# A two-layer graph attention kernel: four of twelve heads turned by TensorE instead of DMA, in a new order of steps

## The reference

```
layer 0: q,k,v = x@Wq+bq, x@Wk+bk, x@Wv+bv          (6 heads of 64)
         p = softmax(q@k.T/sqrt(64) + mask);  y = (p@v)@Wf + bf
         x1 = layernorm(x + y)
layer 1: h = x1@W (12 heads of 32);  th = tanh(h)
         z[i,j] = leaky(th@w_src[i] + th@w_dst[j]);  masked -> -999
         f = elu(softmax(z)@h + b);  g = sigmoid(x1@Hw.T + Hb)
         out = layernorm(x1 + g*f + (1-g)*x1)
```

## Time and profile before

| | |
|---|---|
| three runs | 1217.51, 1220.42, 1220.64 us; median 1220.42 |
| profiled execution | 1217.34 us, span 1215.6 us, mean granted clock 0.974 |
| busy shares of the span | PE 90%, PEld 80%, POOL 82%, ACT 80%, DVE 79% |
| chain that ended last | PE 56%, POOL 15%, issue 14%, DVE 11%, ACT 2%, DMA 1% |
| DMA engines' busy share | 31% |

### The profile page before, as it was taken

One profiled execution on the slowest core, in us unless ns is written; L12 is line 12 of the kernel. 1 busy time (PEld: TensorE's weight loads), 2 busy tenths in 40 slices (PEclk: granted clock), 3 DMA queues, 4 the chain that ended last, 5 costly groups with the idle time before them and its releaser, 6 DMA issues.

```text
span 1215.6 us, 35318 instructions
## 1 busy us (share of the span) xinstructions
PE 1091.1 (90%) x12234; PEld 975.3 (80%) x12297; DVE 962.6 (79%) x1948; ACT 968.6 (80%) x1868; POOL 1000.1 (82%) x813
## 2 busy tenths in 40 slices
PE   4689999999999999999999999999999999999851
PEld 4578888888888888888888888888888888888741
DVE  5567888888888888888888888888888888888843
ACT  5258888888888888888888888888888888888854
POOL 1138898888989888889988888988888898988876
PEclk9799999999999999999999999999999999999975
DMA  4103332223333222333322233332223333223233
GB/s 144 43 17 83 81 90 65 73 68 93 87 86 92 66 68 67 93 87 87 93 66 66 68 93 89 85 93 66 66 74 87 93 87 86 73 67 75 68 66 79
DMA packets 244762, 95.18 MB, mean 78 GB/s; under 512 B 223349, under 2 KB 239738, under 8 KB 244730
## 3 DMA queue, kind: packets, MB, share of 16 engines
q1 hardware_dynamic: 244730, 94.76, 31.2%
HBM read 31.22 MB, written 12.58 MB: 36 GB/s over the span
## 4 chain that ended last, share of the span: by engine, by line
PE 56%; POOL 15%; issue 14%; DVE 11%; ACT 2%; DMA 1%; DVEq 1%; SPq 0%; POOLq 0%; ACTq 0%
PE lin L448 33%; PE zp L545 6%; POOL z L1295 5%; POOL prod L1254 5%; PE fp L570 3%; PE zp L603 3%; PE zp L607 3%; DVE sd L978 2%; PE fp L620 2%; PE fp L573 2%; PE tp L487 2%; DVE y L1073 1%; DVE f L1117 1%; DVE z L1098 1%; ACT th L721 1%
## 5 line engine op out<-in xcount | busy, mean ns | idle before, releaser
L1302 POOL TENSOR_TENSOR p_lo<-z,p_hi 128x1536 f16<-128x1536 f32 x64 | 200.9, 3139 | 0.0
L1295 POOL TENSOR_TENSOR z<-z,z_max 128x1536 f32<-128x1536 f32 x64 | 176.5, 2758 | 9.1 <-DVE z_max L1105 6.1
L784 ACT ACTIVATE z<-zp 128x1536 f32<-128x1536 f32 x64 | 93.1, 1455 | 85.9 <-PE zp L607 85.9
L1254 POOL TENSOR_TENSOR prod<-th,w_sd_rows 128x768 f32<-128x768 f32 x64 | 120.5, 1883 | 14.0 <-ACT th L721 14.0
L620 PE MATMUL fp<-h_part,p1t_hi 128*128 128x33 bf16 x2304 | 110.6, 178 | 19.2 <-DMA p1t_lo<-p_lo 14.8
L620 PEld LDWEIGHTS fp<-h_part,p1t_hi 128*128 128x128 f16 x2304 | 104.4, 96 | 27.2 <-issue 24.1
L1307 POOL TENSOR_TENSOR f<-f,x_kept 128x384 f32<-128x384 f32 x64 | 64.7, 1011 | 73.6 <-DVE f L1124 69.4
L1098 DVE SCALAR_TENSOR_TENSOR z<-zp,z 128x1536 f32<-128x1536 f32 x64 | 112.2, 1753 | 11.0 <-ACT z L784 8.3
L776 ACT ACTIVATE p<-p,p_min 128x128 f32<-128x128 f32 x384 | 118.9, 396 | 0.0
L1105 DVE TENSOR_REDUCE z_max<-z 128x12 f32<-128x1536 f32 x64 | 111.6, 1744 | 0.0
L623 PE MATMUL fp<-h_part,p1t_lo 128*128 128x33 bf16 x1536 | 106.8, 178 | 0.0
(11 more groups left out here) (161 smaller groups left out, 4387.0 us busy)
## 6 DMA issues: line engine op xcount, KB each, us to landing
xt_raw<-x_t SPq DMA_DIRECT2D x32, 384.0 KB, 3.4
x_raw<-x SPq DMA_DIRECT2D x32, 384.0 KB, 3.5
out<-out_tile SPq DMA_DIRECT2D x64, 192.0 KB, 1.9
adj<-adj SPq DMA_DIRECT2D x64, 32.0 KB, 2.8
dst_row<-sd_t SPq DMA_DIRECT2D x64, 9.0 KB
p1t_hi<-p_hi SPq DMA_TRANSPOSE x64, 3.3
p1t_lo<-p_lo SPq DMA_TRANSPOSE x64, 3.3
z<-Wq SPq DMA_DIRECT2D x1, 576.0 KB, 3.5
```

Source lines behind the costliest of these rows:

```text
L784: act.activation(z[:, g, :], zp[:, :, :].rearrange("p b n -> p (b n)"), ACT.Copy)\
L1254: pool.tensor_tensor(prod[:, g, :].rearrange("p (s d) -> p s d", s=2), th[:, g:g + 1, :].to_broadcast([128, 2, D]), rows["w_sd"][:, :].rea ...
L1295: pool.tensor_tensor(zs, zs, z_max[:, g, :].unsqueeze(2).to_broadcast([128, H1, N]), ALU.subtract)\
L1302: pool.tensor_tensor(p1_lo[:, g, :], z[:, g, :], p1_hi[:, g, :], ALU.subtract).then_inc(w1_lo[g].sem, 1)
```

## The change

- Heads 0 to 3 (512 of the 1536 columns) of each graph are transposed by TensorE straight from the float32 weights `z` (`weights1_transposes`, into a `tp` bank), and split on eviction: `turned1_high` on ACT, `turned1_low` on DVE. Heads 4 to 11 go on as before, so `weights1_high`, `weights1_low` and both DMA transposes handle 1024 columns instead of 1536.
- `attend1(g, 0)` waits for `turned1_low`, and `attend1(g, 1)` for the DMAs.
- `z_copy` of the next pair also waits until the transposes have read `z`.
- The step lists of all five engines are in another order, and the banks have other users. On PE `queries_keys(0)` now runs ahead of the late attention steps, `hidden(1)` follows `attend1(0, 2)`, and `gate_rows(0)` is late.

```diff
+PE_HEADS, DMA_HEADS = 4, 8
-LIN_USERS = ("qk0", "pr0", "pr1", "g1", "v0", "qk1", "qk2", "v1", "h0", "h1", "g0")
-TP_USERS = ("pt11", "pt10", "ct0", "ct1", "x1t0", "x1t1", "pt00", "pt01", "sdt")
+LIN_USERS = ("h1", "qk0", "g0", "pr0", "g1", "pr1", "v0", "qk1", "qk2", "v1", "h0")
+TP_USERS = ("pt01", "pt00", "pt11", "sdt", "pt10", "ct0", "ct1", "x1t0", "wt0", "wt1", "x1t1")
-SECOND_BANK = ("pr0", "pr1", "v0", "qk2", "h0", "g0", "pt10", "ct1", "pt00", "pt01")
+SECOND_BANK = ("h1", "g0", "pr0", "g1", "v0", "qk2", "h0", "pt01", "pt11", "ct0", "ct1", "x1t0", "wt1")
...
+                def weights1_transposes(g):
+                    pe.wait_ge(z_exp[g].sem, prev(z_exp[g]))
+                    bank_free(TP_USERS, f"wt{g}")
+                    bank = tp_bank(f"wt{g}")
+                    for i in range(PE_HEADS):
+                        last = pe.transpose(bank[:, N * i:N * (i + 1)], z[:, g, N * i:N * (i + 1)], ident[:, :])
+                    last.then_inc(wt_mm[g].sem, 1)
...
                     if k == 0:
...
+                        pe.wait_ge(wt_lo[g].sem, now(wt_lo[g]))
+                    if k == 1:
                         pe.wait_ge(wt_turned[g].sem, prev(wt_turned[g]))
...
+                    act.wait_ge(wt_mm[g].sem, now(wt_mm[g]))
                     act.activation(z[:, g, :], zp[:, :, :].rearrange("p b n -> p (b n)"), ACT.Copy)\
...
-                    act.activation(p1_hi[:, g, :], z[:, g, :], ACT.Copy).then_inc(w1_hi[g].sem, 1)
+                    act.activation(p1_hi[:, g, :], z[:, g, PE_HEADS * N:], ACT.Copy).then_inc(w1_hi[g].sem, 1)
+
+                def turned1_high(g):
+                    act.wait_ge(wt_mm[g].sem, now(wt_mm[g]))
+                    act.wait_ge(f_mm[g].sem, prev(f_mm[g]))
+                    act.activation(p1t_hi[:, g, 0:PE_HEADS * N], tp_bank(f"wt{g}")[:, :], ACT.Copy)\
+                        .then_inc(wt_hi[g].sem, 1)
...
+                def turned1_low(g):
+                    dve.wait_ge(wt_hi[g].sem, now(wt_hi[g]))
+                    dve.wait_ge(f_mm[g].sem, prev(f_mm[g]))
+                    dve.tensor_tensor(p1t_lo[:, g, 0:PE_HEADS * N], tp_bank(f"wt{g}")[:, :],
+                                      p1t_hi[:, g, 0:PE_HEADS * N], ALU.subtract).then_inc(wt_lo[g].sem, 1)
```

More of the change, by code:

```diff
@@ L626, in attend1 @@
                         last.then_inc(f_mm[g].sem, 1)
+                turn.late(2, attend1, 0, 2)
+                turn.late(1, hidden, 1)
+                turn.late(0, weights0_transposes, 0, 1)
+                turn.late(0, weights0_transposes, 0, 0)
+                turn.late(2, attend1, 1, 0)
+                turn.late(2, attend1, 1, 1)
                 turn.late(2, attend1, 1, 2)
+                turn.step(0, queries_keys, 0)
                 turn.late(0, weights0_transposes, 1, 1)
+                turn.late(1, gate_rows, 0)
+                turn.late(1, source_target_transposes)
+                turn.late(0, attend0, 0)
                 turn.late(0, weights0_transposes, 1, 0)
-                turn.late(0, attend0, 0)
+                turn.late(0, context_transposes, 0)
                 turn.late(1, attention1, 0)
                 turn.late(0, attend0, 1)
-                turn.late(0, context_transposes, 0)
-                turn.step(0, queries_keys, 0)
+                turn.late(0, project, 0)
                 turn.late(0, context_transposes, 1)
-                turn.late(0, project, 0)
                 turn.late(1, attention1, 1)
+                turn.late(1, gate_rows, 1)
                 turn.late(0, project, 1)
-                turn.late(1, gate_rows, 1)
                 turn.step(0, values, 0)
+                turn.step(1, x1_transposes, 0)
                 turn.step(0, queries_keys, 1)
                 turn.step(0, queries_keys, 2)
-                turn.step(1, x1_transposes, 0)
                 turn.step(0, values, 1)
+                turn.step(2, weights1_transposes, 0)
                 turn.step(0, scores, 0)
+                turn.step(2, weights1_transposes, 1)
                 turn.step(1, hidden, 0)
@@ L843, in next_x_high @@
                                    xt_raw[:, :, :].rearrange("p c n -> p (c n)"), ACT.Copy).then_inc(xt_hi_made.sem, 2)
+                turn.late(1, z_copy, 0)
+                turn.late(1, gate_quarter, 0)
                 turn.step(0, queries_keys, 0)
+                turn.late(0, context_high, 1)
+                turn.late(1, hidden_part1, 1)
+                turn.late(1, hidden_part2, 0)
                 turn.late(1, z_copy, 1)
                 turn.late(1, keep_x1, 0)
-                turn.late(1, hidden_part2, 1)
[L849 to L863, removed]
+                turn.late(1, keep_x1, 1)
+                turn.late(1, gate_tanh, 1)
+                turn.late(0, norm0, 0)
+                turn.step(0, value_part1, 0)
+                turn.step(1, x1_high, 0)
+                turn.late(1, z_exponent, 0)
+                turn.step(0, queries_keys, 1)
+                turn.late(1, weights1_high, 0)
+                turn.step(0, queries_keys, 2)
+                turn.late(1, z_exponent, 1)
+                turn.late(1, weights1_high, 1)
+                turn.step(2, turned1_high, 0)
+                turn.late(0, norm0, 1)
+                turn.step(0, value_part1, 1)
+                turn.step(2, turned1_high, 1)
+                turn.late(1, hidden_part2, 1)
                 turn.step(1, hidden_tanh, 0)
                 turn.step(1, x1_high, 1)
+                turn.step(-1, next_x_high)
                 turn.step(0, scores_exp, 0)
-                turn.step(0, value_part2, 1)
+                turn.step(0, value_part2, 0)
                 turn.step(1, hidden_tanh, 1)
+                turn.step(0, weights0_high, 0, 1)
                 turn.step(0, weights0_high, 0, 0)
@@ L1146, in shift_norm1 @@
                         .then_inc(norm1_shift[g].sem, 1)
+                turn.late(0, weights0_low, 1, 0)
+                turn.late(0, context_low, 0)
+                turn.late(2, elu, 1)
+                turn.late(0, context_inverse, 1)
                 turn.late(0, context_norm, 1)
                 turn.late(1, z_leak, 0)
-                turn.late(0, context_low, 0)
-                turn.late(2, elu, 1)
-                turn.late(1, z_maxima, 0)
+                turn.step(0, queries_keys, 0)
+                turn.late(0, add_residual, 0)
                 turn.late(0, context_low, 1)
-                turn.late(0, add_residual, 0)
-                turn.step(0, queries_keys, 0)
                 turn.late(0, stats0, 0)
@@ L1158, in body @@
                 turn.late(0, variance0, 0)
+                turn.late(1, z_maxima, 0)
+                turn.late(0, shift_norm0, 0)
                 turn.late(1, z_leak, 1)
@@ L1203, in body @@
                 turn.late(2, shift_norm1, 1)
-                turn.step(0, context_inverse, 1)
             turns(dve, passed, body, other_weights)
```

127 lines of the change are left out of this document (59 added, 68 removed).

## The result

The changed kernel takes 1210.01 us (median of 4, 1209.52 to 1211.80) against 1219.49 for the kernel before on the same chip: ratio 0.9927, 95% interval 0.9908 to 0.9945. It is faster by 0.7%. The prediction said 1230 and slower, with 0.67; its own range, 1222 to 1244, lies above the time, and only the wide one, 1200 to 1259, holds it.

What follows compares the result with a forecast made beforehand. PE was taken to set the 35.3 us turn: less 2.1, plus 0.9, 0.86 and 0.8, gives 35.8. Over 30 turns +13.5, less 3 at the end: 1227.8 profiled, about 1230 median; own range 1222 to 1244, wide 1200 to 1259.

Steps and rivals of the forecast that it cites:

- The four old stalls: PE's waits before source_target_transposes, attend0(0), project(0) and values(0), 1.44 us a turn as marked, were all to go.
- together 2.1 us a turn: Worth of PE's four old stalls: 1.44 us marked, plus about 0.16 more for each.
- PE has no idle to hide them: Eight added transposes around scores(0) were to cost PE their full 0.88 us a turn.
- Transposes, 0.88 a turn: Eight more float32 transposes on PE, 0.11 us each, counted in full at 0.88 us a turn.
- New stall 1, 0.86: PE waits before context_transposes(0) for the normalised context from DVE: 0.86 us a turn, ends 0.5 and 1.4.
- New stall 2, 0.8: PE waits before attention1(1) for z_leak(0), since both use zp: 0.8 us a turn, ends 0.4 and 1.5.
- Flat rows, 0 to 0.3: PE's attention1(0) needs the flat rows: 0 to 0.3 us of stall, counted at nothing.
- The end of the span, -3: POOL's shorter low parts and the smaller transfer at the program's end were to save about 3 us.
- Median 3.1 above the profiled execution: Median of runs taken as 3.1 us above the profiled execution, so 1227.8 became about 1230.
- POOL's relief, "none of these ends last, so I count nothing": Shorter weights1_low takes 2.1 us a turn off POOL, 31.2 to 29.1; counted at nothing in the turn.
- Rival 1 (faster through the relief): POOL's relief brings work ahead of both new stalls earlier: turn 34.6 us, about 1196 us; chance 0.20.
- Rival 2's place, x1T(1): ACT or DVE holds PE ahead of values(1) and x1T(1): 0.75 us a turn, about 1252 us; chance 0.25.

Runs made afterwards that it cites:

- e4: Changed kernel with each of the four transposes per graph issued twice into the same place, 8 more a turn: 1236.1 us, ratio 1.0142 to the kernel before.
- e1: Changed kernel's new order with all 12 heads transposed by DMA, no TensorE transposes of the weights: 1267.8 us, ratio 1.0402 to the kernel before.
- e2: Kernel before, in its old order, with only the four heads on PE added: 1239.5 us, ratio 1.0167 to the kernel before.
- e11: Changed kernel with attend0(0) moved before source_target_transposes and gate_rows(0) after it on PE, two DVE feature steps moved up: 1198.1 us, ratio 0.9837.
- e9: e3 with mask0_bias and deviation0(1) ahead of weights1_low(0) on POOL, moments0(1) and variance0(1) earlier on DVE: 1259.7 us, ratio 1.0347.
- e8: Changed kernel with only ACT's weights1_high back at all 12 heads' width: 1220.3 us, ratio 1.0001 to the kernel before.
- e3: Changed kernel with POOL's weights1_low and ACT's weights1_high back at all 12 heads' width: 1278.9 us, ratio 1.0500 to the kernel before.
- e7: e1 with deviation0(1) ahead of weights1_low(0) on POOL, moments0(1) and variance0(1) ahead of queries_keys(2) on DVE: 1287.0 us, ratio 1.0548.
- e10: e1 with mask0_bias and deviation0(1) ahead of weights1_low(0) on POOL, moments0(1) and variance0(1) earlier on DVE: 1286.2 us, ratio 1.0569.

## Why the prediction was wrong

*The four old stalls go:* right, all four. *Their worth, "together 2.1 us a turn", and with it "PE has no idle to hide them" of the added transposes:* this is the step that failed. I took only the rows that carry a bracket naming an engine. Two gaps of the old order were left inside what I called PE's own work. One is after `source_target_transposes`: 538.86 to 539.31, 0.45 for two transposes that take 0.12 in the changed kernel (539.46 to 539.58); 0.33, of which 0.17 is marked, as "issue"; what holds PE there no row says. The other is ahead of `scores(0)`; the timeline of PE in the kernel before:

```profile
526.91 0.34 PE L448 MATMUL lin<-Wv_hi,xt_lo 128*128 128x384 f32 x1
527.32 0.33 PE L545 MATMUL zp<-k_hi,q_hi 64*128 64x128 f32 x2
```

One such matmul has its successor 0.17 later, here it is 0.41: 0.24 of waiting for the last k_lo, without a bracket. Now the first transposes of the weights stand there, ahead of `scores(0)`, in place of x1T(0), and `scores(0)` starts 2.21 us after the last matmul of `queries_keys(2)` (522.75 to 524.96) with hardly a gap. The gaps were 2.1 + 0.57 = 2.67 us a turn, and the turn without stalls is 35.32 - 2.67 + 0.88 = 33.53, not 34.1. Measured: 35.23 less 0.72, 0.68, 0.12 and the 0.15 before `queries_keys(1)` is 33.56.

The forecast turn was 34.1 + 0.86 + 0.8 = 35.76, the measured one 35.23, 0.53 less. The gaps make -0.57 of it. The two new stalls came out 0.26 shorter than forecast and two waits counted at nothing cost 0.27, so these cancel, which is luck. Over 29 turns 0.53 is 15 us. The first, irregular turn is 3 us shorter than a forecast turn (32.80), and ahead of it 0.8 us were added: together the 17.3 us between the 1227.8 forecast for the profiled execution and the 1210.46 measured.

*Transposes, 0.88 a turn:* right as PE's own time (0.53 + 0.41 in the trace, 0.82 for eight more in e4); but the first four stand in a gap, as e1 and e2 show. *New stall 1, 0.86:* measured 0.72. *New stall 2, 0.8:* 0.68. The Trainium skill, "Perfetto Trace Analysis", Optimization Strategy, says that a gap that repeats on the engine that should be saturated can mean too little room in SBUF or PSUM for the next tile. The trace agrees for this one: `attention1(1)` waits each turn for z_leak(0) to free `zp`. It doesn't for stall 1, which e11 removed by order alone. *Flat rows, 0 to 0.3:* 0.12. *The end of the span, -3:* measured -3.0. *Median 3.1 above the profiled execution:* not so for the changed kernel, 1210.01 against 1210.46; that is 3 of the 20 us between 1230 and 1210.

*POOL's relief, "none of these ends last, so I count nothing":* the sum was not hurt by it, since the stalls were counted with POOL at its new load, but as a statement it was wrong. In the old order the relief is worth nothing in the turn (e2). In the new one its loss costs 1.5 us a turn (e9 against the changed kernel, ACT's part included) and 2.3 where POOL's and DVE's lists are left as they were (e3). The new order needs it. *Rival 1 (faster through the relief):* it asked for less than 1.2 us of new stalls together; they were 1.40. The faster time came from the gaps that the forecast had left out and from the first turn, not from this mechanism. *Rival 2's place, x1T(1), with 0.2 to 0.3 in hand:* the reserve was about as small as said; it did not break at the change's load, but did with 0.45 us more on ACT (e8: 0.29 us of wait by starts, some 9 us in all) and with 1.0 more on POOL as well (e3: 1.27).

Still open: why the first, irregular turn gained 3.0 us, which is close to half of the measured gain, and what holds PE in the 0.33 us behind `source_target_transposes`. No run parted these.

## What to carry to other kernels

Measure an engine's idle by the distance between starts of neighbouring instructions, not by the gaps the profile puts a name to: two unnamed gaps of 0.33 and 0.24 us a turn made the sign of this forecast. A step on an engine with spare time is not free if small steps that others wait for stand behind it in its list, so a new order and the loads that it was made for have to be judged together: here each alone cost 2% to 4% and both gained 0.7%. Once the sum of waits is known by place, put a long independent step into the longest one; that alone gave 0.9% more here, less than the stall was long, because the next wait behind it grew. And look at the start and the end of a program before crediting its loop: here the loop's regular turns gave only a quarter of the gain.

## What was not expected of the hardware

In e3 PE stood 1.09 us idle once a turn, then worked on transposes, scores and many small matmuls, and the granted clock was 0.50 from 518 to 521 us and 0.79 in the microsecond after. The length of the idle alone does not tell whether this happens. In e3 itself the turns from 129 to 240 us had nearly the same idle (1.12 at 216.05) and stayed at 1.00; from 240 us on the clock fell in each turn. In e7 it fell after two shorter idles, 0.46 and 0.80 (PE's timeline, then the windows), in e10 after one of 1.37 (0.61 in the 4.4 us behind it). e1, with recorded idles of 0.36, 0.63, 0.29, 0.73 and more in each turn, and e9 with 0.50, 0.72 and more stayed at 1.00 in the middle.

```profile
522.43 0.33 PE L550 MATMUL zp<-k_hi,q_hi 64*128 64x128 f32 x2 [0.46 <-DVE p L1047]
...
524.45 0.24 PE L633 MATMUL fp<-h_part,p1t_hi 128*128 128x33 bf16 x3 [0.80 <-DMA p1t_lo<-p_lo]
```
```profile
526.00:527.00 1.00, 1.00 (x11) 1.00 (x8) 0.71 (x2) 0.00 (x0) 1.00 (x2) 0.50 0.67 153
```

So in this kernel a stall of PE of about a microsecond can bring a slow stretch with it, which made e3's turn 0.5 us or so longer than the stall and the waits alone.
